# Attention kernel of one pre-norm layer: heads packed into row tiles of TensorE, row maxima taken two heads at a time, the fourth score tile issued behind the value matmuls

## What is computed

```python
Q = einsum('bsd,ed->bse', x, Wq).reshape(b, s, 16, 16).transpose(0, 2, 1, 3)   # K, V alike
Q = _rope(Q); K = _rope(K)
scores = einsum('bhqd,bhkd->bhqk', Q, K) / math.sqrt(16)
scores = where(causal_mask, -inf, scores)
out = einsum('bhqk,bhkd->bhqd', softmax(scores, axis=-1), V)
return einsum('bsd,ed->bse', out.transpose(0, 2, 1, 3).reshape(b, s, d), Wo)
...
x = x + _L0_attn_ref(_layernorm(x), Wq, Wk, Wv, Wo)
x = x + relu(_layernorm(x) @ w1 + b1) @ w2 + b2
```

## Time and profile before

| | |
|---|---|
| median of 3 runs | 2350.91 us (2350.78 to 2351.55) |
| profiled execution | 2349.89 us, its span 2348.2 us |
| busy: TensorE | 2216.7 us, 94% of the span |
| busy: VectorE | 1977.1 us, 84% |
| busy: ScalarE | 1460.6 us, 62% |
| busy: GpSimd | 697.8 us, 30% |
| mean granted TensorE clock | 0.968 of full speed |

### The profile page before, as it was taken

The page is one execution under the profiler, slowest core; times in us unless marked ns, Lnnn a source line. Parts: engine busy times, 40 slices in busy tenths (PEclk is TensorE's granted clock), DMA queues, the critical chain, the costliest instruction groups (busy, mean ns, idle before and its releaser), DMA issues. The chain is left out here.

```text
span 2348.2 us, 43338 instructions
## 1 busy us (share of the span) xinstructions
PE 2216.7 (94%) x13984; PEld 897.4 (38%) x13984; DVE 1977.1 (84%) x4854; ACT 1460.6 (62%) x3140; POOL 697.8 (30%) x1361
## 2 busy tenths in 40 slices
PE   6776889999999999999999999999999878999999
PEld 3443123333333333333333333333333215767676
DVE  8997989999999999999999999999999305666665
ACT  5663047777777777777777777777777772232322
POOL 8996411222222232231223222132222221101010
PEclk9997579999999999999999999999999998999999
DMA  5668020303032130303302031230303011121210
GB/s 185 220 215 234 21 49 20 59 24 60 15 60 44 34 64 19 60 20 58 60 20 63 15 59 36 43 64 19 60 6 64 6 54 48 58 76 58 70 60 28
DMA packets 131167, 142.55 MB, mean 61 GB/s; under 512 B 13856, under 2 KB 113696, under 8 KB 130720
## 3 DMA queue, kind: packets, MB, share of 16 engines
q1 hardware_dynamic: 130976, 140.24, 23.4%
HBM read 81.20 MB, written 58.72 MB: 60 GB/s over the span
## 5 line engine op out<-in xcount | busy, mean ns | idle before, releaser
L825 ACT ACTIVATE s_prob<-s_ps 128x512 f32<-128x512 f32 (+3 forms) x2560 | 1167.5, 543 | 386.3 <-PE s_ps L660 386.2
L732 DVE TENSOR_REDUCE s_part<-s_ps 128x1 f32<-128x512 f32 x1536 | 946.8, 678 | 60.0 <-PE s_ps L646 56.4
L646 PE MATMUL s_ps<-mk,mq 112*128 112x512 f16 (+3 forms) x2560 | 896.4, 359 | 25.8 <-DVEq L784 17.7
L660 PE MATMUL s_ps<-aq,ak 113*128 113x512 f16 (+3 forms) x2560 | 868.4, 351 | 29.2 <-ACT s_prob L825 14.3
L675 PE MATMUL s_ps<-s_prob,s_v 128*32 128x512 f32 (+3 forms) x5120 | 600.0, 541 | 0.4 <-POOL s_prob L857 0.4
L660 PEld LDWEIGHTS s_ps<-aq,ak 113*128 113x128 f16 x2560 | 244.6, 97 | 706.3 <-ACT s_prob L825 574.5
L728 DVE CUSTOM_DVE_ANT_0 s_ps<-s_ps,mask_sb 128x512 f32<-128x512 f32 (+3 forms) x1024 | 469.8, 522 | 43.0 <-PE s_ps L646 34.6
L857 POOL TENSOR_SCALAR_AFFINE_SELECT s_prob<-s_prob 128x128 f32<-128x128 f32 x1024 | 285.9, 294 | 496.9 <-ACT s_prob L825 479.3
L646 PEld LDWEIGHTS s_ps<-mk,mq 112*128 112x128 f16 x2560 | 252.2, 99 | 233.7 <-DVE s_part L732 46.7
L862 POOL TENSOR_TENSOR s_yt<-s_ot,s_rsum 128x512 f32<-128x512 f32 x64 | 67.1, 1048 | 460.2 <-DVE s_rsum L752 460.2
L675 PEld LDWEIGHTS s_ps<-s_prob,s_v 128*32 128x32 f32 x5120 | 100.7, 108 | 224.9 <-ACT s_prob L825 134.4
(11 more groups left out here) (85 smaller groups left out, 1672.1 us busy)
## 6 DMA issues: line engine op xcount, KB each, us to landing
v_scratch<-s_vst SPq DMA_DIRECT2D x32, 512.0 KB, 3.9
s_v<-v_scratch SPq DMA_DIRECT2D x16, 1024.0 KB, 11.6
aq<-qk_scratch SPq DMA_DIRECT2D x96, 128.0 KB, 4.7
ak<-qk_scratch SPq DMA_DIRECT2D x96, 128.0 KB, 7.3
s_xin<-x SPq DMA_DIRECT2D x16, 512.0 KB, 4.4
qk_scratch<-s_r_lo SPq DMA_DIRECT2D x64, 128.0 KB, 2.3
qk_scratch<-s_r_hi SPq DMA_DIRECT2D x64, 128.0 KB, 2.5
att_scratch<-s_y_lo SPq DMA_DIRECT2D x64, 128.0 KB, 1.9
```

What stands on the lines that cost most here:

```text
L646: nc.tensor.matmul(ps[:, bank, 0:w], mq[0:MROWS, p, j, qt * P:(qt + 1) * P], mk[0:MROWS, p, kc * CH:kc * CH + w], start=True, stop=True).t ...
L660: nc.tensor.matmul(ps[:, s_bank(s, j), q0:CH], ak[0:AROWS, p, j // 2, kb * P:(kb + 1) * P], aq[0:AROWS, p, j, c * CH + q0:(c + 1) * CH], s ...
L732: nc.vector.tensor_reduce(largest, ps[:, bank, 0:w], AX.X, ALU.max).then_inc(m_read, 1)
L825: nc.scalar.activation(prob[:, s % 2, j, q0:CH], ps[:, s_bank(s, j), q0:CH], ACT.Exp, scale=1.0 / (SQK * DK ** 0.5)).then_inc(p_done, 1)
```

## The change

Five things change together.

1. Row tiles. `mq` loses its dimension of heads, `aq` keeps two of four. A score matmul now reads 64 partitions (0 to 63 for even heads, 64 to 127 for odd ones), and a maximum matmul reads 32 (32 for each of the four heads). The compiled matmuls are tiles of 64 x 128 and 32 x 128 of the array at those rows; before all were 128 x 128 at row 0.
2. Pairs of maxima. `max_pair` issues two matmuls into two neighbouring banks with one wait and one semaphore increment. The four banks are now two pairs (NM = 2). In full steps VectorE reduces both banks with one instruction of 1024 elements; where the mask is added there are still two instructions, with one increment behind the second.
3. Order on TensorE: first pair, scores 0, 1, 2, value products of the step before, score 3, second pair.
4. `xin`, `att_hi` and `att_lo` of stage 3 get memory of their own and no longer lie in `mq`; a wait on SyncE in the last iteration goes.
5. The two smaller buffers are cleared by shorter memsets on GpSimd at the start of stage 1.

```diff
-MROWS = 32 * (G - 1) + DK
-AROWS = HROWS + MAXROW + 1
+MROWS = 32
+NP = G // 2
...
-        self.mq = ctx.enter_context(nc.sbuf_tensor("mq", [P, 2, G, S], F16))
+        self.mq = ctx.enter_context(nc.sbuf_tensor("mq", [P, 2, S], F16))
...
-        self.aq = ctx.enter_context(nc.sbuf_tensor("aq", [P, 2, G, S], F16))
+        self.aq = ctx.enter_context(nc.sbuf_tensor("aq", [P, 2, NP, S], F16))
...
-        M_BANK, NM, S_BANK, SB, O_BANK = 0, 4, 4, 3, 7
+        M_BANK, NM, S_BANK, SB, O_BANK = 0, 2, 4, 3, 7
...
-                sp.wait_ge(m_ready, M_BEFORE + i * M_ITER)
...
-                nc.tensor.matmul(ps[:, bank, 0:w], mq[0:MROWS, p, j, qt * P:(qt + 1) * P],
-                                 mk[0:MROWS, p, kc * CH:kc * CH + w], start=True, stop=True).then_inc(m_ready, 1)
+                for jj in range(2):
+                    row = MROWS * (2 * pair + jj)
+                    last = nc.tensor.matmul(ps[:, bank + jj, 0:w], mq[row:row + MROWS, p, qt * P:(qt + 1) * P],
+                                            mk[row:row + MROWS, p, kc * CH:kc * CH + w], start=True, stop=True)
+                last.then_inc(m_ready, 1)
...
+                rows = slice(HROWS * (j % 2), HROWS * (j % 2 + 1))
+                nc.tensor.matmul(ps[:, s_bank(s, j), q0:CH], ak[rows, p, j // 2, kb * P:(kb + 1) * P],
+                                 aq[rows, p, j // 2, c * CH + q0:(c + 1) * CH], start=True, stop=True
...
-                    for j in range(G):
+                    if not last:
...
+                        max_pair(1 - p, s, 0, m_use(i, s, 0), m_bank(p, s, 0))
+                    for j in range(SB):
                         score_tile(i, p, s, j)
-                        if not last:
-                            if s == 0 and j == 0:
-                                pe.wait_ge(m_in[1 - p], 128 * (use + (1 if p else 0) + 1))
-                            max_tile(1 - p, s, j, m_use(i, s, j), m_bank(p, s, j))
                     if s > 0:
                         pv_step(i, p, s - 1)
                     elif not first:
                         pv_step(i - 1, 1 - p, NS - 1)
+                    score_tile(i, p, s, G - 1)
+                    if not last:
+                        max_pair(1 - p, s, 1, m_use(i, s, 1), m_bank(p, s, 1))
...
-                if kc == qt // TPC:
+                if kc < qt // TPC:
+                    nc.vector.tensor_reduce(part[:, qt // 8, 2 * pair:2 * pair + 2, qt % 8, kc], ps[:, bank:bank + 2, 0:w],
+                                            AX.X, ALU.max).then_inc(m_read, 1)
+                    return
+                for jj in range(2):
...
-                        if j == 1:
+                        if pair == 0:
```

More of the change, by code:

```diff
@@ L77, in load_m @@
     for j in range(G):
-        rows = slice(32 * j, 32 * j + DK)
-        for qk, dst in ((0, ops.mq[rows, p, j]), (1, ops.mk[rows, p])):
+        rows = slice(MROWS * j, MROWS * j + DK)
+        for qk, dst in ((0, ops.mq[rows, p]), (1, ops.mk[rows, p])):
             src = qk_d[bass.ds(i, 1), 0, qk, DK * j:DK * (j + 1), :].rearrange("a r t -> (a r) t")
@@ L89, in load_a @@
                 rows = slice(HROWS * jj + DK * r, HROWS * jj + DK * (r + 1))
[L90 removed]
+                dst = (ops.ak if qk else ops.aq)[rows, p]
                 src = qk_d[bass.ds(i, 1), hl, qk].rearrange("a (jp jj r) t -> (a jj) r jp t", jj=2, r=DK)
@@ L640, in _, with max_pair @@
         def _(pe):
-            def max_tile(p, s, j, use, bank):
+            def max_pair(p, s, pair, use, bank):
                 qt, kc = qtile(s)
@@ L704, in _ @@
             for s in range(NS):
-                for j in range(G):
-                    use = G * s + j + (s > ROWS1_STEP)
-                    max_tile(0, s, j, use, M_BANK + use % NM)
+                for pair in range(NP):
+                    use = NP * s + pair + (s > ROWS1_STEP)
+                    max_pair(0, s, pair, use, M_BANK + 2 * (use % NM))
                 if s == ROWS1_STEP:
-                    use = G * (s + 1)
-                    max_rows(0, use, M_BANK + use % NM, 1)
+                    use = NP * (s + 1)
+                    max_rows(0, use, M_BANK + 2 * (use % NM), 1)
             iteration(0, 0, 0, first=True)
@@ L719, in _, with max_of_pair @@
         def _(dve):
-            def max_of_tile(s, j, use, bank, first=False):
+            def max_of_pair(s, pair, use, bank):
                 qt, kc = qtile(s)
@@ L723, in max_of_tile @@
                 dve.wait_ge(m_ready, use + 1)
-                largest = part[:, qt // 8, j, qt % 8, kc:kc + 1]
-                if kc == qt // TPC:
-                    dve.sem_inc(masking, 1)
-                    nc.vector.tensor_tensor_reduce(out=ps[:, bank, 0:w], in0=ps[:, bank, 0:w], in1=mask[:, CH - w:CH],
-                                                   scale=1.0, scalar=MASKED, op0=ALU.add, op1=ALU.max,
-                                                   accum_out=largest).then_inc(m_read, 1)
-                else:
-                    nc.vector.tensor_reduce(largest, ps[:, bank, 0:w], AX.X, ALU.max).then_inc(m_read, 1)
+                if kc < qt // TPC:
[3 more added lines that the diff above has]
+                for jj in range(2):
+                    dve.sem_inc(masking, 1)
+                    last = nc.vector.tensor_tensor_reduce(
+                        out=ps[:, bank + jj, 0:w], in0=ps[:, bank + jj, 0:w], in1=mask[:, CH - w:CH], scale=1.0,
+                        scalar=MASKED, op0=ALU.add, op1=ALU.max,
+                        accum_out=part[:, qt // 8, 2 * pair + jj, qt % 8, kc:kc + 1])
+                last.then_inc(m_read, 1)
             def max_of_half(half, read):
@@ L759, in iteration @@
                 for s in range(NS):
-                    for j in range(G):
+                    for pair in range(NP):
                         if not last:
-                            max_of_tile(s, j, m_use(i, s, j), m_bank(p, s, j))
-                        if j == 1:
+                            max_of_pair(s, pair, m_use(i, s, pair), m_bank(p, s, pair))
+                        if pair == 0:
                             for c in range(NC):
```

45 lines of the change are left out of this document (22 added, 23 removed).

## The result

The changed kernel takes 2425.04 us (median of 4 runs, 2407.97 to 2432.08) against 2350.85: a ratio of 1.0305, 95% interval 1.0251 to 1.0359. It is slower by 3%, and outside the predicted range (2285 to 2402).

A forecast was written before the change was run, and what follows sets the result against it. TensorE was taken as the bound, 2.84 us a full step. Attention iterations +1 us and the rest +1 on the median of 2350.9 gave 2353 us, put at 2350; range 2285 to 2402.

The forecast's parts named there:

- the rival of the clock: TensorE's granted clock falls to the lower level: +1 us a step, 2900 us; chance 0.08 together with no overlap.
- the missing overlap: Rival: row-tiled matmuls don't overlap, full step 3.02 us, 2455 us in all; chance 0.08 together with the lower clock.
- Row tiles side by side: On TensorE, two matmuls on different rows were taken to cost one slot of 0.22 us.
- not one slot: Rival: a pair's second matmul starts 0.10 us later, iteration 3 to 4 us longer, 2400 us; chance 0.17.
- The ring: Chain of score 2, value products, score 3, its exponential, back to score 2: 2.45 us a step, unchanged by the reorder.
- this slack: Room in the two-step loop before VectorE delays TensorE: 0.11 - 2x, so 0.11 us or -0.07.
- The loop over two slots: With two slots, a first pair waits for VectorE's reading; transposes make the step two later some 0.6 us longer.
- A pair's reduction: On VectorE, reducing both banks at once was taken to cost 1.13 us, so 2.27 us a step instead of 2.40.
- x: What TensorE loses between a maximum and a score, tiles of different size: 0 to 0.09 us.
- its sum: Work of VectorE landing on the path, 6.7 to 8.5 us an iteration, giving iterations of 100.2 to 102.0 us.
- The `max_rows` stall: In steps 5 and 13 it takes one of two slots, delaying the next first pair 1.2 to 1.4 us each.
- The last iteration: Iteration without maxima: 93.5 + 0.8 against 91.2 us, +3, as the fourth score waits behind masks and copies.

The follow-up runs named there:

- e3: Changed kernel with only the score matmuls back over all 113 rows (128 x 128 tiles); 2406.95 us, ratio 1.0235 to the kernel before.
- e11: Changed kernel with only the maximum matmuls reading 112 rows again, one after the other; 2502.12 us, ratio 1.0643 to the kernel before.
- e5: Changed kernel plus, in the last iteration from step 6, one unread 128-row matmul in place of each pair of maxima; 2399.99 us, ratio 1.0207.
- e7: Changed kernel plus unread 128-row matmuls in the last iteration and ahead of pairs in diagonal steps and steps 0 to 6 of all iterations; 2476.56 us.
- e4: Kernel before with only the fourth score and its maximum moved behind the value products; 2384.81 us, ratio 1.0136.
- e1: Changed kernel with the fourth score back in front of the value products, row tiles and pairs kept; 2739.07 us, ratio 1.1652 to the kernel before.
- e8: Changed kernel with 113-row scores in the order of before, row-tiled pairs of maxima behind scores 0 and 2; 2360.45 us, ratio 1.003.
- e9: Changed kernel with 113-row scores in the order of before, row-tiled pairs of maxima behind scores 1 and 3; 2361.45 us, ratio 1.0041.
- e2: Changed kernel with four single slots for the maxima instead of two pairs, same order; 2438.62 us, ratio 1.0339 to the kernel before.
- e6: Changed kernel plus, in the last iteration from step 6, two unread 32-row matmuls side by side replacing each pair; 2409.65 us, ratio 1.0251.

## Why the prediction was wrong

**The step that failed** is the rival of the clock: "The new step lies near the last iteration, so I expect 1.00." The comparison was with an iteration of before in which every score fills a slot of its own. With row tiles the two scores of a pair share one, so in the last iteration TensorE had less to do in the same ring, and the clock went to 0.50 for much of it. By e3 and e11 the row-tiled scores are what lets it fall; that it is the smaller amount of work about them fits e5 to e7 but isn't shown apart from the tiles themselves. It was priced with the missing overlap at 0.08 in all, and as all or nothing (2900 us); what came is a part of the time at the lower level. In the profiled execution it costs 41 us in iterations 0 to 14 (8 of them in iteration 0) and some 24 in the end of the last (104.14 against 80.02 in e3, which has the same order), 65 of the 82. From the medians it is less direct: e3 less 15 x 2.55 would be 2369, measured 2425, 56 us. The rest is a matter of size, below.

**Row tiles side by side: right.** And more: four maxima share a slot, as do two scores, so the rival "not one slot" didn't happen by itself. e11 made it, and its price holds: 3 to 4 us for 0.1 us was forecast, 7.6 for 0.22 measured.

**The ring: right in kind**, 2.39 instead of 2.45 us, but only every second plain step has that length; the others take 2.62, held by VectorE. The prediction had this slack at -0.07 us for two steps at worst, measured are -0.23.

**The loop over two slots: right in kind.** Waits of the first pair for `part`, steps of 3.0 to 3.2 us where a transpose was in VectorE's way, 0.6 to 0.8 over plain ones.

**Sizes.** A pair's reduction costs 1.13 where VectorE alone sets the pace, as TensorE's starts in the pass ahead show, and 1.18 on average over four in plain steps, where one of them waits for its pair:

```profile
239.61 0.61 PE L647 MATMUL s_ps<-mk,mq 32*128 32x512 f16 x2 [0.53 <-DVE s_part L731]
240.74 0.60 PE L647 MATMUL s_ps<-mk,mq 32*128 32x512 f16 x2 [0.52 <-DVE s_part L731]
```

```profile
707.96 4.75 DVE L731 TENSOR_REDUCE s_part<-s_ps 128x2 f32<-128x1024 f32 x4 [0.59 <-PE s_ps L647]
```

x is 0.10, 0.01 over its upper end. (The two bounds that the prediction gives beside x, 100.4 and 102.2 us, don't follow from its sum, which is 100.2 to 102.0.) The `max_rows` stall is 1.50, forecast as 1.2 to 1.4. The iteration at full clock is 101.85, in the range of 100.2 to 102.0, by its upper end; 15 of them cost 12 us where 1 was taken.

**The parts, at full clock, for an iteration:** order +2.15 (e4), maxima in row-tiled pairs +1.22 (e3 less e4), scores in row tiles -2.55 (changed less e3). The differences hold in this sequence only: e1 shows that without the order the others would be far worse. The prediction says that the reorder "leaves the ring as it was"; alone, on the kernel before, it costs 32 us, all of it outside the full steps.

**The last iteration**: +3 was forecast, 28.8 came, of which the clock is most; with the same order at a clock of 1.00 (e3, e4) it is +0.8.

No version here beats the kernel before. e8 and e9 come within 0.3 to 0.4% of it and gain nothing in an iteration, since both find a new bound right under the old: changes of tile in e8, the ring through score 3 in e9. What they lose lies mostly in the low clock of iteration 0 and ahead of it.

## What to carry to other kernels

Before you shorten TensorE's work in a step that another engine's ring will then bound, ask what the granted clock does with the idle time. A stretch of before at 1.00 proves nothing for one in which the scores take half the slots. And where the clock falls, compare steps at a clock of 1.00 with such steps, and not whole iterations. Count changes of tile size as work (0.10 us each here), and count what stands between a score and the exponential that frees its bank.

## What the hardware showed that was not expected

- The last iteration, with the same order and steps of 2.40 and 2.39 us, keeps a granted clock of 1.00 with scores of 113 rows (e3, end 80.02 us) and falls to 0.50 for its last 57 us with scores of 64 rows two at a time (e11, end 98.28 us).
- How long it stays low differs widely between profiled executions of the same code: the end of that iteration took 104.14, 98.28 and 82.24 us (changed, e11, e2).
- With unread matmuls in it the clock stays at 1.00, be they of 128 rows (e5, 83.59 us) or of 32 (e6, 85.26). Whether it is the shared slot or another trait of the scores' tiles that matters was not separated further.
- Four matmuls of 32 rows each, into four banks, take 0.39 us together, as one does; the last starts 0.01 us behind the first.
